# Moving the context's projections and transpose between slots of a software-pipelined attention and mixture-of-experts kernel, with VectorE's order changed to match

## The reference

```
n  = layernorm(x)
y  = causal_attention(n Wq + bq, n Wk + bk, n Wv + bv)          # 16 heads of 8 channels
y += attention(n Wcq + bcq, ctx Wck + bck, ctx Wcv + bcv)        # to the context, no mask
x1 = x + y Wp + bp
m  = layernorm(x1)
shared = (silu(m W1^T) * (m W2^T)) W3^T                          # hidden size 512
score  = sigmoid(m Wr^T); the top 2 of 8 experts by score + bias
routed = sum over them of score * ((silu(m A_e^T) * (m B_e^T)) C_e^T)   # hidden size 128 each
out = x1 + shared + routed
```

## Time and profile before

| | |
|---|---|
| time, median of 3 runs | 451.9 us (451.32 to 452.56) |
| time of the profiled execution | 452.91 us |
| its span, first to last instruction | 451.2 us |
| its mean granted TensorE clock | 0.966 of full speed |
| TensorE matmuls busy | 401.8 us, 89% of the span |
| VectorE busy | 351.0 us, 78% |
| ScalarE busy | 195.8 us, 43% |
| GpSimd busy | 77.4 us, 17% |

### The profile page before, as it was taken

The page is one execution under the profiler, slowest core; times in us unless marked ns, Lnnn a source line. Parts: engine busy times, 40 slices in busy tenths (PEclk is TensorE's granted clock), DMA queues, the critical chain, the costliest instruction groups (busy, mean ns, idle before and its releaser), DMA issues.

```text
span 451.2 us, 10427 instructions
## 1 busy us (share of the span) xinstructions
PE 401.8 (89%) x3759; PEld 298.0 (66%) x3759; DVE 351.0 (78%) x1186; ACT 195.8 (43%) x326; POOL 77.4 (17%) x139
## 2 busy tenths in 40 slices
PE   0579998999899989999899998999889998998986
PEld 0457565667577667767577756767577766765986
DVE  4477676855898877996989787987889788884877
ACT  5135554453433554355443544553444553444221
POOL 4012001400222021210222013110231003201120
PEclk9999899967899998999999989999899999999999
DMA  5631101110201111110201110110101110000000
GB/s 145 198 103 39 54 25 61 58 31 1 84 0 55 48 42 41 41 41 17 81 0 52 47 54 27 52 47 6 64 8 49 42 59 15 1 25 0 2 13 12
DMA packets 28478, 19.63 MB, mean 44 GB/s; under 512 B 6680, under 2 KB 26272, under 8 KB 28448
## 3 DMA queue, kind: packets, MB, share of 16 engines
q1 hardware_dynamic: 27296, 19.02, 13.0%
q10 hardware_dynamic: 1152, 0.20, 0.4%
HBM read 5.58 MB, written 1.05 MB: 15 GB/s over the span
## 4 chain that ended last, share of the span: by engine, by line
PE 51%; DVE 26%; ACT 12%; issue 8%; DMA 1%; SPq 1%; DVEq 0%; POOL 0%; ACTq 0%; POOLq 0%
PE Y L574 10%; ACT probs L793 8%; PE Bk L426 8%; PE Cb L426 6%; DVE masked_s L1030 6%; PE S L450 5%; PE A L426 4%; DVE act L915 4%; DVE shifts L1036 4%; PE Cb L657 3%; PE S L468 3%; ACT th L773 3%; DVE qs L1005 2%; DVE acc L955 2%; PE Y L541 2%
## 5 line engine op out<-in xcount | busy, mean ns | idle before, releaser
L793 ACT ACTIVATE probs<-S 128x1024 f32<-128x1024 f32 (+1 forms) x128 | 112.3, 917 | 54.1 <-PE S L452 53.4
L780 ACT COPY yT<-Y 128x256 f32<-128x256 f32 x64 | 23.9, 373 | 133.8 <-PE Y L574 133.8
L1036 DVE TENSOR_REDUCE shifts<-S 128x4 f32<-128x1024 f32 x64 | 75.2, 1216 | 1.0 <-PE S L468 0.7
L574 PE MATMUL Y<-probs,vs 128*32 128x256 f32 (+1 forms) x1024 | 67.4, 384 | 9.2 <-DVE qs L1005 6.9
L1030 DVE CUSTOM_DVE_ANT_0 masked_s<-S,later_keys 128x256 f32<-128x256 f32 (+1 forms) x256 | 73.4, 352 | 1.4 <-PE S L464 1.3
L915 DVE SCALAR_TENSOR_TENSOR act<-th,A 128x512 f32<-128x512 f32 x42 | 28.7, 683 | 38.2 <-ACT th L773 38.1
L450 PE MATMUL S<-qs,qk 32*128 32x256 f32 x256 | 46.5, 398 | 10.1 <-DVE shifts L1030 7.6
L1080 POOL TENSOR_SCALAR_AFFINE_SELECT probs<-probs 128x1024 f32<-128x1024 f32 x32 | 35.2, 1100 | 108.5 <-ACT probs L793 108.5
L574 PEld LDWEIGHTS Y<-probs,vs 128*32 128x32 f32 x1024 | 27.9, 114 | 34.2 <-DVE qs L1005 17.4
L426 PEld LDWEIGHTS Bk<-w3T,hid 128*128 128x128 f32 x336 | 41.5, 194 | 13.0 <-DVE hid L924 12.2
L426 PE MATMUL Bk<-w3T,hid 128*128 128x128 f32 x336 | 49.2, 290 | 0.6 <-DVE hid L924 0.6
(11 more groups left out here) (148 smaller groups left out, 689.5 us busy)
## 6 DMA issues: line engine op xcount, KB each, us to landing
qk<-nat SPq DMA_DIRECT2D x192, 64.0 KB, 1.9
xin<-in_x_dram SPq DMA_DIRECT2D x8, 128.0 KB, 2.3
w_raw<-in_L_ffn_w_dram SPq DMA_DIRECT2D x4, 256.0 KB
xres<-in_x_dram SPq DMA_DIRECT2D x8, 128.0 KB, 2.3
out_dram<-acc SPq DMA_DIRECT2D x8, 128.0 KB, 1.8
cin<-in_ctx_dram SPq DMA_DIRECT2D x8, 64.0 KB, 2.0
w_raw<-in_L_ffn_shared_w_dram SPq DMA_DIRECT2D x4, 128.0 KB
w_raw<-in_L_ffn_w_dram SPq DMA_DIRECT2D x1, 512.0 KB
```

Of the source, the lines that this page charges most:

```text
L574: mm = nc.tensor.matmul(Y[QUAD * j:QUAD * (j + 1), q0:T], vs[:, kind, kt, GH * g + j, :], probs[u % 2][:, j, kt * T:(kt + 1) * T - q0], st ...
L793: nc.scalar.activation(probs[s % 2][:, hs, 0:kept(s)], S[:, hs, 0:kept(s)], ACT.Exp, scale=SCALE).then_inc(exped[s], 1)
L1036: nc.vector.tensor_reduce(dst.rearrange("p q j -> p j q"), S[:, hs, :].rearrange("p j (q k) -> p j q k", q=NT), AX_X, ALU.max).then_inc(re ...
```

## The change

The context's projections ("qkc", the queries and keys of the attention to the context) go from EARLY of slot 6 to EARLY of slot 7. The context's transpose ("cT") goes from LATE of slot 4 to EARLY of slot 4, where TensorE now does it between the exp pass and shift_rows. The projection "v" goes from EARLY of slot 5 to LATE of slot 4. On VectorE, qs now comes ahead of activate in every slot with a pair; the statistics of the next input go from slot 7 to the head of slot 6, and the comparison of the router's scores to right behind them; "qkc" is read between the two halves of slot 7's maxima; the choice of the experts goes to the end of slot 7. GpSimd does both of the router's steps and the inverse deviation of the next input in slot 6. No instruction is added or taken away, and no size changes.

```diff
-EARLY = [("xT", 1), ("tokens3", -1), ("yT", -1), ("vc", 0), None, ("v", 1), ("qkc", 1), None]
-LATE = [("tokens2", -1), ("qk", 1), ("out", -1), ("x2T", -1), ("cT", 1), ("route", -1), ("tokens0", 0), ("tokens1", 0)]
+EARLY = [("xT", 1), ("tokens3", -1), ("yT", -1), ("vc", 0), ("cT", 1), None, None, ("qkc", 1)]
+LATE = [("tokens2", -1), ("qk", 1), ("out", -1), ("x2T", -1), ("v", 1), ("route", -1), ("tokens0", 0), ("tokens1", 0)]
...
                     else:
+                        bank_c(turn, EARLY[s])
                         shift_rows(turn, s)
...
                     pr = pair_of(s)
-                    if pr and turn.has(pr[1]):
-                        activate(turn, pr)
-                    if s == 7 and turn.has(2):
+                    if s == 6 and turn.has(2):
                         wait(dve, x_in, turn.n(2, 16, 16))
                         normalise(turn, 2, ln1, 0, 6, xin, stats1, mv1, xn, rstd1_ready, rstd1, True)
+                    if s == 6 and turn.has(-1):
+                        compare(turn, -1)
...
                         nc.vector.tensor_tensor(qs[:, u % 2, :], qk[:, u, 0, :].bitcast(F32), Y[:, :],
                                                 ALU.subtract).then_inc(shifted[u], 1)
                     if pr and turn.has(pr[1]):
+                        activate(turn, pr)
+                    if pr and turn.has(pr[1]):
                         times_h2(turn, pr)
-                    if late:
+                    if late and s < 7:
                         from_bank_c(turn, EARLY[s])
...
+                    if s == 7 and not turn.has(o):
+                        from_bank_c(turn, EARLY[s])
                     if turn.has(o):
                         for half in range(2):
                             hs = slice(2 * half, 2 * half + 2)
+                            if s == 7 and half == 1:
+                                from_bank_c(turn, EARLY[s])
...
-                    if s == 6 and turn.has(-1):
-                        compare(turn, -1)
-                    if s == 7 and turn.has(-1):
-                        choose(turn, -1)
...
                     from_bank_c(turn, LATE[s])
+                    if s == 7 and turn.has(-1):
+                        choose(turn, -1)
...
-                    if s in (6, 7) and turn.has(-1):
-                        route(turn, -1, s - 6)
-                    if s == 7 and turn.has(2):
-                        rstd(turn, 2, ln1, 4, 6, mv1, var1, rstd1, rstd1_ready)
+                    if s == 6:
+                        if turn.has(-1):
+                            route(turn, -1, 0)
+                        if turn.has(2):
+                            rstd(turn, 2, ln1, 4, 6, mv1, var1, rstd1, rstd1_ready)
+                        if turn.has(-1):
+                            route(turn, -1, 1)
```

## The result

The changed kernel takes 495.8 us (median of 4 runs, 488.8 to 496.6) against 452.2 us (median of 4 runs) before. Executions that took over 1.5% longer than their kernel's fastest, two of these four and one of the four before, are left out of the ratio, which compares 492.0 with 451.9 us: it is 1.089, with a 95% interval of 1.072 to 1.106. Slower was forecast, but 470 us and at most 481. The profiled execution took 495.23 us with a span of 493.5 us.

What follows compares the result with a forecast made beforehand. One loop over TensorE and VectorE in each slot was taken to bound the kernel. Five full turns at +3.2 us, ends +0.8 and one dip 1.0 took 452.9 to 470.7, so 470 us was predicted, range 458 to 481.

Steps and rivals of the forecast that it cites:

- the chain from x2T over cT to qs: Slot 4: cT waits for x2T's read and qs for cT's read, so qs starts 1.37 us later.
- slot 6's gain: Slot 6: without qkc ahead of hidden 1 and the maxima, the maxima start 1.19 us earlier.
- The rival that ended faster: Filling VectorE's 2.53 us idle time in slot 6 gives 1.2 us or more a turn; 440 us, chance 0.05.
- the one in which the order is free: times_h2 is not in the loop, so only slots 4 and 5 cost; 459 us, chance 0.15.
- a dip: A fall of TensorE's granted clock, priced at about 1.0 us from two turns; one more added to the sum.
- the rival with more dips: One more clock dip in each of 8 to 10 places, 1.0 us each; 479 us, chance 0.17.
- The third rival: More clock dips because TensorE waits longer: 8 to 10 more at 1.0 us each; 479 us, chance 0.17.
- The chain without dips: A full turn's change from slots 0 to 3, 4 and 5, 6 and 7: +1.8 + 1.5 - 0.1 = +3.2 us.
- Slots 0 to 3: qs ahead of activate puts activate into the loop; +1.8 us a turn, between +1.3 and +2.2.
- Slot 7: qkc waits for tokens0 and stands ahead of shift_rows; the stretch between maxima ends grows from 4.52 to 5.61, +1.1 us.
- Slots 4 and 5: cT's wait in slot 4 and activate behind qs in slot 5; +1.5 us a turn, between +1.0 and +2.0.
- turn 7: No cT, v or qkc; slots 1 to 3 cost up to 1.6, slots 5 and 6 give some back; +0.6 us.

Runs made afterwards that it cites:

- e9: Changed kernel with activate put back ahead of qs and four short matmuls without use on TensorE ahead of slot 4's cT; 463.2 us.
- e1: Changed kernel with four short matmuls without use on TensorE ahead of the context's transpose in slot 4; 476.3 us, ratio 1.058 to before.
- e4: Kernel before with qkc in slot 7 and the moves belonging to it, activate still ahead of qs, cT and v unmoved; 455.2 us, ratio 1.010.
- e5: Changed kernel with activate put back ahead of qs; 476.8 us, ratio 1.053 to before.
- e3: Kernel before with only cT moved to the middle of slot 4 and v to slot 4's end; 473.0 us.
- e2: Kernel before with only VectorE's order changed, qs ahead of activate in each slot with a pair; 480.4 us, ratio 1.066.
- e6: Kernel before without its short matmuls without use in slot 4; 457.0 us, ratio 1.011.
- e10: Changed kernel with x2T read by VectorE ahead of slot 3's sum instead of behind it; 478.6 us.
- e7: Kernel before with only the input's statistics and the comparison moved to slot 6's head, and GpSimd's order to match; 448.6 us, ratio 0.992.

## Why the prediction was wrong

**What held.** The direction, and each place. In slot 4 the forecast of the chain from x2T over cT to qs was +1.37 us and it is +1.42; slot 6's gain was -1.19 and is -1.15, with the statistics and the comparison hidden as worked out. VectorE now idles ahead of qs in every slot with a pair. TensorE's waits in a turn grew from 2.5 to 6.1 us, near the forecast of 5.7. The rival that ended faster, and the one in which the order is free, fell: the order costs 2.6 us a turn within the change (e9 against e1). The later transfers were not late (slot 2 in e4).

**The step that failed: the clock.** The prediction gave a dip 1.0 us, the difference of two turns of before, and added one of them; the rival with more dips had the same price and 0.17. Both the count and the price were wrong. Behind slot 4 the clock stays at 1.2 GHz for some 10 us, over the part of the turn in which TensorE sets the pace, and costs 3.6 us (e1), 3.9 (e5 against e9, 55.43 - 51.54) or 3.7 (e3). It did so in each of turns 2 to 5, and in turn 6 for 6.8 us. The dip from which the price was read lay in slots 7 and 0 and lasts 3.4 us. What such a short one costs goes by its place: 1.0 us where it reached slot 0 (7.44 instead of 6.46 us before), nothing in slot 7 of e1. The third rival had the mechanism, more dips, but with this price its 479 us fell short too. A dip of the long kind stood in the trace of before, in turn 1 from 93 to 107 us, in the clock line's slices of 6 and 7 tenths; I saw it and let it fall out of the sum.

**Terms that were too small.** The chain without dips is +4.7 us a turn, where the forecast had +3.2. Slots 0 to 3 cost 2.45 instead of 1.8: times_h2 behind activate waits for its end, 0.71 from start to start instead of the 0.60 of independent neighbours, which is 0.11 more a slot, and in slot 0 it was 0.82 (in slot 5 0.81). Slot 7 costs 1.61 instead of 1.1. Slots 4 and 5 cost 1.74 without the dip (e1) instead of 1.5. The last interval, from slot 5 of turn 6 to slot 5 of turn 7, takes 51.19 us instead of 47.63, +3.6, where I had +0.6 for turn 7. By slots it is -1.1 in slot 6, +2.3 in slot 7, +2.0 in slots 0 to 3 and +0.4 in slot 5: slot 7 took only 3.87 before, as turn 6 has no statistics of a next input to lose there, and turn 7 pays the order like the others.

**The sum again.** From slot 5 of turn 1 to slot 5 of turn 7 the kernel before takes 299.2 us and the changed one 339.5, +40.3. Five turns of chain are 5 x 4.68 = 23.4. Dips: the changed kernel's five turns are 288.3 us, 17.8 above 5 x 54.11; those of before 251.55, 4.4 above 5 x 49.43; so 13.4. The last interval gives 3.6. These make 40.4; the parts are differences of the same rows, so that they add up is no check of the price of a dip, for which e1, e5 with e9, and e3 stand. Of the 42.3 us between the two spans 2.7 more lie ahead of slot 5 of turn 1, and the end gives 0.7 back. Against the forecast of +17.8 (16.8 and one dip), dips make 12.4 of what was missing, the chain 7.4, the last interval 3.0, and fill and ends the rest.

**The clock, by rows.** In the changed kernel the clock fell to 1.2 GHz after TensorE had waited 0.30 and 0.95 us within slot 4, and it stayed there over ten microseconds in which TensorE's matmuls were busy all the time (the window from 271 to 281 us). Four short matmuls in that wait kept it full behind slot 4 in all five turns (e1, e9). The Trainium skill, "TensorE: Matmul & The Clock Gate", Part 1, says that the throttled state is the default and activity releases it. The fall agrees with that; that a TensorE without a gap does not bring it back for 10 us is not what a reader of busy time would take from it.

**What stays open.** What decides whether a wait brings a long dip. With the same 0.95 us it came in two of five turns in e3 and in five of five in e5 and in the changed kernel, and once each in e2, e6 and e10 without it; the kernel before has its own in turn 1, behind waits of 0.58 and 0.41 us. Nor is it length alone. In slot 7 of the changed kernel TensorE stops even longer, for 1.18 us in each of the turns 1 to 5, and no dip begins there:

```profile
237.70 0.63 PE L657 MATMUL Cb<-ident,yT 128*128 128x128 f32 x4 [1.18 <-DVE nat L863]
```

No run moved a stop in time without changing anything else, so that it hangs on when the stop comes, or on which matmuls surround it, is not excluded. What e1, e9 and e10 show is that filling or removing this stop takes the long dips out of most turns. Nor do the runs settle why the dip behind slot 4 lasts so much longer than the one in slot 7.

## What to carry to other kernels

When VectorE idles ahead of an instruction, ask what that instruction would be waiting behind if it were moved: activate sat in idle time, and moved behind qs it stood in the loop that both engines share, at its full length plus the hand-over to the instruction that reads its result. Before an item moves forward in a queue of single-bank users, look up when the bank's last reader finishes; a stop of 1 us of TensorE's in-order queue costs what lies behind it and may cost the clock, as in slot 4 here. Price a change of the clock's dips by the longest dip that the trace shows and by the place where it would fall, not by the nearest; and filling VectorE's idle time with independent work, without touching the order of what is in the loop, was the part that paid (e7).

## What the runs showed of the hardware

The granted clock's record can read 1.00 while TensorE runs slow: in e6, from 49 to 59 us, with four matmuls of line 468 at 0.80 us instead of 0.50. The same page of the Trainium skill, Part 1, warns that the trace's clock events have been seen to be unreliable; this trace agrees. The fill of the kernel before shows the same: the record has no dip ahead of 45 us, and yet the matmuls below, of one group, differ. So take the durations of a known group beside the record.

```profile
36.71 0.78 PE L426 MATMUL Cb<-xT,wx_hi 128*128 128x256 f32 x2
...
60.20 0.51 PE L426 MATMUL Cb<-xT,wx_hi 128*128 128x256 f32 x2
```

Once down behind slot 4, the clock stayed at 1.2 GHz for some 10 us although matmuls ran back to back (0.51 granted, TensorE busy 10.00 of 10.00 us from 271 to 281 in the changed kernel).
